# Gate folded into the attention output product, chunk ramps in two fp32r parts, feed-forward normalisations spread over the fills

## The reference, cut to what matters

```
x = x + _L0_attn_ref(_layernorm(x, axis=-1), ...)   # SSD in chunks of 128, then silu(h@w1)*(h@w3)@w2
x = x + _L0_ffn_ref(_layernorm(x, axis=-1), L0_ffn_factors, L0_ffn_bias)
x = x + _L1_attn_ref(_layernorm(x, axis=-1), L1_attn_W_Q, L1_attn_W_K, L1_attn_W_V, L1_attn_W_O)
x = x + _L1_ffn_ref(_layernorm(x, axis=-1), L1_ffn_gate_w, L1_ffn_w1, L1_ffn_w3, L1_ffn_w2)

# in _L1_attn_ref
attn_out = jnp.einsum('bqnh,nhd->bqd', z, W_O)
# in _L1_ffn_ref
router_logits = x @ gate_w.T
probs = jax.nn.softmax(router_logits, axis=-1)
topk_vals, topk_idx = jax.lax.top_k(probs, TOP_K)
topk_vals = topk_vals / jnp.sum(topk_vals, axis=-1, keepdims=True)
a = jax.nn.silu(g) * u          # width 704
out = jnp.einsum('te,teh->th', combine, y)
```

## Time and profile before

| | us |
|---|---|
| three runs | 554.78, 559.87, 560.05 |
| median of them | 559.87 |
| profiled execution, its own time | 557.6 |
| span of the profiled execution | 555.8 |
| PE busy in it | 510.9 (92%) |
| DVE / ACT / POOL busy | 356.6 / 278.4 / 179.4 |

### The profile page before, as it was taken

How to read it: one execution, slowest core, us unless ns; L and a number is a source line. 1 busy time by engine, 2 the same in 40 slices (tenths; PEclk the granted TensorE clock), 3 DMA queues, 4 the chain that set the end, 5 groups by cost and what they waited for, 6 DMA issues and landing times.

```text
span 555.8 us, 9970 instructions
## 1 busy us (share of the span) xinstructions
PE 510.9 (92%) x3285; PEld 419.0 (75%) x3286; DVE 356.6 (64%) x871; ACT 278.4 (50%) x529; POOL 179.4 (32%) x236
## 2 busy tenths in 40 slices
PE   3998989989989998989999998798999999999994
PEld 1647877878968876767778886576888888888883
DVE  5875778557457336556668675456777777777761
ACT  1594544216123265556565563025666666666651
POOL 3016539971032032332223110310433333333332
PEclk9999999999999999899999999878999999999998
DMA  8999010000010069000000005851122222222111
GB/s 321 401 337 291 1 43 35 1 0 1 1 38 1 0 243 397 34 29 20 11 32 12 20 20 190 340 172 30 20 39 38 38 38 38 38 38 38 28 17 22
DMA packets 25813, 47.47 MB, mean 85 GB/s; under 512 B 2224, under 2 KB 21168, under 8 KB 25392
## 3 DMA queue, kind: packets, MB, share of 16 engines
q1 hardware_dynamic: 21408, 41.76, 21.2%
q0 software_dynamic: 4080, 5.15, 6.3%
q10 hardware_dynamic: 288, 0.08, 0.1%
HBM read 32.01 MB, written 14.98 MB: 85 GB/s over the span
## 4 chain that ended last, share of the span: by engine, by line
PE 77%; DVE 10%; ACT 5%; issue 5%; POOL 1%; DMA 1%; POOLq 0%; ACTq 0%; DVEq 0%
PE ps L1757 16%; PE ps L1777 11%; PE ps L1550 6%; PE ps L1648 5%; PE ps L1633 4%; PE ps L1448 4%; PE ps L1663 4%; PE ps L1606 4%; PE ps L1572 4%; PE ps L1765 3%; PE ps L1682 2%; PE ps L1610 2%; PE ps L1414 2%; PE ps L1532 1%; ACT work L777 1%
## 5 line engine op out<-in xcount | busy, mean ns | idle before, releaser
L1757 PE MATMUL ps<-split,xsT 128*128 128x512 f32 (+1 forms) x414 | 95.4, 384 | 1.1 <-DVE split L1355 1.0
L1757 PEld LDWEIGHTS ps<-split,xsT 128*128 128x128 f32 x414 | 75.8, 191 | 14.2 <-issue 1.2
L1355 DVE TENSOR_TENSOR split<-early,split 128x1408 fp32r<-128x1408 f32 x46 | 72.8, 1622 | 7.6 <-ACT split L843 7.2
L1777 PE MATMUL ps<-mid,work 128*128 x276 | 63.4, 379 | 0.8 <-ACT work L832 0.8
L843 ACT CAST split<-early 128x1408 fp32r x46 | 62.6, 1365 | 0.9 <-issue 0.9
L609 POOL TENSOR_TENSOR rstd<-mhalf 128x1 f32<-128x1 f32 x23 | 22.8, 993 | 120.4 <-ACT work L839 120.4
L1205 DVE TENSOR_REDUCE nmax<-ps 128x1 f32<-128x128 f32 (+7 forms) x64 | 45.4, 750 | 22.2 <-PE ps L1633 22.0
L1777 PEld LDWEIGHTS ps<-mid,work 128*128 128x128 f32 x276 | 52.0, 190 | 7.0 <-issue 1.0
L1337 DVE TENSOR_TENSOR work<-work,ps 128x704 f32<-128x704 f32 x23 | 20.4, 887 | 43.0 <-PE ps L1757 43.0
L828 ACT ACTIVATE work<-ps 128x704 f32<-128x704 f32 x22 | 16.7, 758 | 50.2 <-PE ps L1757 50.2
L777 ACT ACTIVATE work<-ps,nmax 128x128 f32<-128x128 f32 (+7 forms) x48 | 35.9, 750 | 2.9 <-DVE nmax L1205 2.9
(11 more groups left out here) (256 smaller groups left out, 1141.0 us busy)
## 6 DMA issues: line engine op xcount, KB each, us to landing
early<-m_w SPq DMA_DIRECT2D x16, 704.0 KB, 9.6
expert_in<-pad SPq DMA_DIRECT2D x8, 1040.0 KB, 12.4
mid<-m_w SPq DMA_DIRECT2D x8, 640.0 KB, 8.9
work<-expert_in SPq DMA_DIRECT2D x23, 130.0 KB, 2.9
early<-factors SPq DMA_DIRECT2D x1, 2048.0 KB, 11.6
early<-wq SPq DMA_DIRECT2D x1, 2048.0 KB, 16.3
mid<-f_w SPq DMA_DIRECT2D x1, 2048.0 KB, 20.6
rows<-x_in SPq DMA_DIRECT2D x4, 256.0 KB, 3.8
```

The costliest lines, as they stand in the source:

```text
L1355: V.tensor_tensor(lo, expert_w(e, w), hi.bitcast(F32), ALU.subtract).then_inc(s_wlo[w], 1)
L1757: last = mm(up_flat[:, c0:c1], xsT[px][b][:, k, :], split_w[pw][:, k, c0:c1], start=(k == 0 and px == pw), stop=(k == KD - 1 and px == 1))
L1777: last = mm(ps[:, 6, 0:D], eaT[:, b, c, :], we[:, c, :], start=(c == 0), stop=(c == IB - 1))
```

## The change

It has four parts.

1. **Gate folded.** The router's logits are linear in the layer norm of x, and x after attention is x before plus z·W_O. So the gate weights are centred over the 256 features (PE `gate_sums`, DVE `centre_gate`), W_O is transposed (8 transposes, copied by ACT), and the product of W_O with the centred gate (8 columns per 128 rows) is written behind W_O as columns 256 to 263 of `wo_m`. The part of the logits that comes from x before attention (`base_logit`) is made for all 8 tiles from the transposed normalised rows that the q, k and v projection holds (48 fp32r products of 8 columns) and scaled by the standard deviation. All this stands in the 24 fills of the projection at q = 13, 15, 17, 19 and 21, and the first `scores` waits for it. Then `attention_out` has 264 columns and its last 8 are logits; `route_transposed`, the ACT copy, `route_logits`, the maximum and the softmax go. `route_choice` follows `route_variance` at once (rel 3) on unscaled logits, `route_normalise`, the difference of the two chosen logits times rstd, and `route_slots` come at rel 0 behind the row maxima, ACT takes one exponential of two columns, and `route_weights` comes at rel 1. `route_counts` stands at rel 0 ahead of `attended`. The `keep_busy` runs at the end change from 8, 16, 14, 24 to 8, 20, 20.
2. **Split ramps.** The ramp and its two 0/1 matrices are fp32r: POOL makes a high and a low half (512 elements for 256 before) from a split `dA` (2 more DVE operations before `s_dtv` = 4), and the two fp32 products of each chunk's `front` become two fp32r products each. Two copies on DVE at the start make `sums_r`.
3. **Normalisations tile by tile.** In `swiglu` one tile is normalised behind each of the fills f = 1 to 4, in both groups.
4. **Expert padding gone.** The last of the six transposes and of the six down products of each expert tile uses 64 rows, and the zero fills (DVE L1374 and one on POOL) and their semaphores go.

```diff
@@ decay_ramp, POOL
-                nc.gpsimd.tensor_tensor(by_head(ramp[:, c % 2]), le_m.unsqueeze(1).broadcast_to([P, H_SSD, P]),
-                                        along(dts[1][:, c, :]), ALU.mult).then_inc(s_ramp, 1)
+                nc.gpsimd.tensor_tensor(ramp[c % 2].rearrange("p a (h l) -> p (a h) l", h=H_SSD),
+                                        le_m.unsqueeze(1).broadcast_to([P, 2 * H_SSD, P]),
...
@@ DVE, dA
+            link(V.tensor_copy(da_split[:, :, 0, :], dts[1]))
+            V.tensor_tensor(da_split[:, :, 1, :], dts[1], da_split[:, :, 0, :].bitcast(F32),
+                            ALU.subtract).then_inc(s_dtv, 1)
@@ front, PE
-                mm(ps[:, 2, 0:2 * P], gt_m, rmp, start=True, stop=False)
+                for part in range(2):
+                    mm(ps[:, 2, 0:2 * P], sums_r[:, 0, :], rmp[:, part, :], start=(part == 0), stop=False)
                 mm(ps[:, 2, 0:2 * P], ident_b[:, :], neg_s[:, :], start=False, stop=True)
-                mm(ps[:, 2, 2 * P:4 * P], ones, rmp, start=True, stop=True).then_inc(s_front_seg, 1)
+                for part in range(2):
+                    last = mm(ps[:, 2, 2 * P:4 * P], sums_r[:, 1, :], rmp[:, part, :], start=(part == 0), stop=(part == 1))
+                last.then_inc(s_front_seg, 1)
@@ swiglu, DVE
-                    if g == 0 and f == 1:
-                        normalise(PH_FFN, xn, 1)
+                    if 1 <= f <= GT:
+                        normalise(*((PH_FFN, xn, 1) if g == 0 else (PH_FAC, x, 0)), tiles=(f - 1,))
...
-            normalise(PH_FAC, x, 0)
             swiglu(1)
@@ fills of the projection, DVE and PE
+                if q == 14:
+                    centre_gate()
+                if q == FILLS - 3:
+                    read_gate_fold()
...
+            def gate_folded():
+
+                pe.wait_ge(s_woT, 1)
+                for c in range(QB):
+                    for k in range(KD):
+                        mm(ps[:, 0, c * E:(c + 1) * E], woT[:, k, c * P:(c + 1) * P], gate_sb[:, k, :],
+                           start=(k == 0), stop=(k == KD - 1))
+                for t in range(TT):
+                    at = (QB + t) * E
+                    for part, (pw, ph) in enumerate(W_PARTS):
+                        for k in range(KD):
+                            last = mm(ps[:, 0, at:at + E], hT_split[ph][:, k, t * P:(t + 1) * P], gate_r[:, pw, k, :],
+                                      start=(part == 0 and k == 0), stop=(part == 2 and k == KD - 1))
+                last.then_inc(s_fold, 1)
...
+                if q == 13:
+                    gate_sums()
+                if q == 15:
+                    wo_transposed()
+                if q == 19:
+                    gate_folded()
@@ scores, PE
+                if m == 0:
+                    pe.wait_ge(s_folded, 1)
@@ route_choice, DVE
-                dve.wait_ge(s_lexp, t + 1)
-                link(V.reciprocal(rs[2][:, t:t + 1], rs[1][:, t:t + 1]))
-                link(V.tensor_scalar(prob_e[:, t, :], prob_e[:, t, :], rs[2][:, t:t + 1], None, ALU.mult))
-                link(V.max(top_v[:, t, :], prob_e[:, t, :]))
+                link(V.tensor_tensor(rank_e[:, t, :], ps[:, at, D:D + E], base_logit[:, t, :], ALU.add))
+                link(V.max(top_v[:, t, :], rank_e[:, t, :]))
...
@@ attention_out, PE
-                    last = mm(ps[:, 6 + i % 2, 0:D], zT[:, c, :], wo_sb[:, c, :], start=(c == 0), stop=(c == QB - 1))
+                    last = mm(ps[:, 6 + i % 2, 0:D + E], zT[:, c, :], wo_m[:, c, :], start=(c == 0),
+                              stop=(c == QB - 1))
@@ expert weights, ACT
-            act.wait_ge(s_lg, TT)
+            act.wait_ge(s_lexp, TT)
@@ expert_aT, PE (expert_down alike)
+                    w = P if c < IB - 1 else ILAST
+                    last = nc.tensor.transpose(ps[0:w, 4 + c // 4, (c % 4) * P:(c % 4 + 1) * P],
+                                               ea[:, b, c * P:c * P + w], ident)
```

More of the change, by code:

```diff
@@ L120, in build @@
         fw2_lo = view(overlay("ffn_w2_lo", 2 * KD * FF, FB * D), 0, FB, D)
+        ramp = [view(overlay(f"ramp{b}", E * IB * D - (2 - b) * 2 * H_SSD * P, 2 * H_SSD * P), 0, 2, H_SSD * P)
+                for b in range(2)]
         mid = sb("mid", E * IB * D)
@@ L823, in _ @@
                     attend(2 * m + 1)
+                if rel == 0 and i >= 2:
+                    logits_exp(i - 2)
             def expert_silu(i):
@@ L1292, in _ @@
                     probs_feature_major(2 * m - 2)
-                if rel == 0 and i >= 2:
-                    route_normalise(i - 2)
-                if rel == 1 and i >= 2:
-                    route_choice(i - 2)
                 if m < STEPS:
```

154 lines of the change are left out of this document (80 added, 74 removed).

## The result

The changed kernel takes 568.36 us (median of 4 runs, 566.76 to 569.99); the kernel before, in the runs beside it, takes 557.61 (4 runs). The ratio is 1.0185, 95% interval 1.0142 to 1.0227: 1.9% slower. The profiled execution has 566.76 us. I had forecast 553.5. A kernel's runs fall in groups by their mean granted clock (before: 554.1 to 555.9 us at 0.99 in 8 of its 35 runs, nearly all others at 557.5 to 561.5 with 0.98), so a median of few runs also says how many of them fell in which group.

A forecast was written before the change was run, and what follows sets the result against it. PE was taken to bound the chunk loop and projection, and DVE, ACT or SP order the feed-forward, attention and tail. Terms -2.5 - 1.5 + 8.0 - 4.5 - 2.5 - 1.1 = -4.1 gave 553.5 us; range 546.5 to 560.5.

The forecast's parts named there:

- Chunk ramps, -2.5: Chunk loop: split fp32r ramp products save 2.7 us over seven chunks, less 0.2 at the start; net -2.5 us.
- +0.2 for the start: Start of chunk loop: added DVE operations and copies delay the last convolution and silu by at most about 0.4; +0.2 taken.
- Normalisations, -1.5: Feed-forward: normalising tile by tile removes PE's first wait (-1.3 us) and 0.2 of the second's 1.80; net -1.5 us.
- the wait I had named as next: Feed-forward, second normalisation wait: ACT stands 2.20 us waiting for POOL's sum of factors, which the change does not move.
- Folding, +8.0: Projection: 68 small records (7.0 us), 8 transposes (0.9) and a wait (0.1) add in full on PE; +8.0 us.
- my fifth case: Projection: small products cost a quarter of the assumed price, 68 records 1.7 us; total 548.2 us, chance 0.05.
- Routing, tiles 0 to 5, -4.5: Attention: less PE work (3.4 us) and PE's routing waits gone, together 5.5, less 0.5 for each wide tile; net -4.5 us.
- what I gave back to DVE: Attention's two wide tiles: DVE is nearly the bound, so each gives back 0.5 us of the 5.5 saved.
- The fourth case: Attention: the routing choice holds up DVE's row maxima, 6 x 1.3 = 7.8 us late; total 564.9 us, chance 0.10.
- Tail, -2.5: Tail: ACT's start 2.0 us sooner, slot tile another 2.0 sooner, against 1.5 for a low PE clock; net -2.5 us.
- the 1.5 that I had added for a low clock: Tail: PE stands longer before the first expert products, so one stretch at half clock costs 1.5 us.
- Expert tiles, -1.1: Expert tiles: the narrower last transpose saves 0.05 us in each of 23, the down product keeps its time; -1.1 us.

The follow-up runs named there:

- parts 2 and 3 alone: The kernel before with only split ramps and tile-by-tile normalisations, without folding or the expert padding change: 555.12 us (12 runs), ratio 0.9951 to the kernel before.

## Why the prediction was wrong, step by step

**What bounds the kernel.** Right for the projection, where the products added cost in full. Wrong in what "counts in full" was taken to mean: the product's own duration. In these runs it also counted by what happened to the clock and to the weight loads beside it.

**Chunk ramps, -2.5.** Measured +1.3 in the traces. The saving of a chunk was right (0.39 forecast, 4.20 - 3.82 = 0.38). Two terms failed. I took +0.2 for the start and asked of POOL only whether it has time inside the loop. POOL's first two ramps run beside the last convolutions, on the path, and DVE paid the whole 0.85 us that they grew. The two operations that split `dA` are 0.42 more. With the 0.41 that came before the ramps, from the first products and not from the change, the convolutions end 1.7 us later, and the loop starts 1.5 later. The Trainium skill's page "SBUF — State Buffer", section "SBUF: two separate sides", says of DVE and GpSimd that the pair of ports they share is an exclusive lock, also for a DVE operation with two inputs in SBUF beside a GpSimd one that reads SBUF, and that the other blocks for the whole instruction. Both kinds stand here, and the 9.60 against 8.75 beside 2.92 against 2.07 agrees. The other term was the first chunk at half clock, some 1.5 us, which was in no case of mine. From the ramp product of the second chunk to that of the third it is 48.88 - 44.81 = 4.07 us, where the kernel before has 45.86 - 43.30 = 2.56; then 4.08 against 4.20, and the four after that save 1.5 together: 1.5 + 1.5 - 0.1 - 1.5 = 1.4 late, and the first fill of the feed-forward 1.3. Over runs parts 2 and 3 together are 0.5% faster than before, 2.7 us by the ratio and 3.8 by the medians, where I had forecast 4.0. That this is near is luck: by the traces the two stages together give 0.5 us, and no trace shows the rest to be theirs.

**Normalisations, -1.5.** Measured -1.8. Right, with the wait I had named as next.

**Folding, +8.0.** Measured +14.1 for the stage. The price of a small product was right (0.112 against 0.1025), and the cheap rule of my fifth case was wrong here. What failed is that 64 of them stand in a row. At 0.107 to 0.112 each they are 7.1 us; they took 202.62 - 192.50 = 10.1, and the big products behind them, at half clock, some 1.8 more: 4.8, and dealing them out gave 4.7. Another 0.65 is a low clock at the start of the projection, which came and went between traces of kernels that do not differ there. Without both the stage grew by 8.6, near the 8.0 of the sum. I had used the clock only for pauses of PE; here PE was busy all the time.

**Routing, tiles 0 to 5, -4.5.** Measured -6.3, in sign and mechanism right. Of it 1.0 is a low clock after pauses at 222 to 225 us in the kernel before, which the folded kernels do not have: from the output product of tile 0 to that of tile 1 the kernel before takes 16.08 us and parts 2 and 3 alone, without the low clock, 15.05. The rest, 5.2, is near the 5.5 of my sum without what I gave back to DVE. The wide steps gave nothing back.

**The fourth case** forecast 564.9, nearest to what came, but by a mechanism that did not occur: PE waits for no row maximum that it did not wait for before. A number near the result is no evidence for its story.

**Tail, -2.5.** Measured -3.8. ACT's start against the first weight load came 1.7 us sooner (forecast 2.0), the slot tile another 2.1 (forecast 2.0), and the 1.5 that I had added for a low clock was not there: the first expert product takes 4.48 us in both.

**Expert tiles, -1.1.** Measured +5.6 in the traces of before and after, +7.9 over runs, and +7.2 between the traces with and without part 4 in the changed kernel (from the first expert product to the end 185.8 and 178.6 us; the kernel before has 180.1, with its clock at 0.67 from 384 to 388 us). "The down product has the same columns and keeps its time" is the sentence that failed, and it cost more than any other. The columns stayed the same, and still the load of 64 rows and the next one of 128 each came 0.33 us late, 0.34 net in a tile, which over 22 tiles is 7.5. The Trainium skill says on its page "TensorE: Matmul & The Clock Gate", section "Step-by-step: what each phase is for", that loads are pulled ahead of running products when the row groups do not conflict, or into the background buffer. That sentence makes loads of weights a thing to ask about, but it does not foretell these pauses: the loads of 128 rows use the same rows as the product ahead of them and show none. The other half of the sum, 0.05 us saved in the transposes, failed as well: six take 0.57 us from the first of them to the up product in both kernels, where I had taken 0.66, and the narrow one is no quicker.

**Range.** It ended at 560.5. Its slow end had only the costs of waits and of DVE in it. Each of the three misses has a question that I did not ask: what runs on DVE while POOL makes the first ramps, what does PE's clock do with this mix of products, what does a new shape do to its neighbours.

## What to carry to other kernels

A shape that is new in a stream of equal products is priced with its neighbours: here one product over 64 rows among products over 128 cost 0.34 us in each tile where 0.05 was to be saved, and cutting the padding away bought nothing. A long run of products with few columns was not only slow by itself, the clock halved in it and for the products behind; dealt out between wide products it cost its own time. A sum that comes out near the time is checked stage by stage before it counts as right. When work is taken off a path that ends in a queue, look at what is queued ahead of the transfer that releases the next stage: here the gain was there, but only to be had with one store moved.

## What the runs showed of the hardware that was not expected

- A product over 64 rows between fp32 products over 128: 0.33 us ahead of its weight load and 0.33 ahead of the next one of 128 rows, 0.34 us net, in 22 tiles of the changed kernel and in 22 of the kernel before with that edit alone.
- Transposes of 64 columns instead of 128 as the sixth of six: 0.57 us for the six either way.
- Clock down to 0.50 (1.2 GHz) inside an unbroken run of 8-column products, with PE busy without a gap; at 1.00 with 16 of them between blocks of 6 records of 512 columns; at 0.50 again with 2 products of 256 columns after every 6.
- Twelve two-input DVE operations took 0.85 us longer (9.60 for 8.75) where POOL's work beside them took 0.85 longer (2.92 for 2.07).
